# Normalising rows inside the mix: ScalarE with a scale and a bias per row in place of VectorE

## What is computed

```
h      = bn2(conv1d(relu(bn1(conv1(x))), 17 taps));  x_conv = relu(h + x)
s      = x @ w_se.T + b_se                       # 3 coordinates of a node
A      = exp(-|s_n - s_m|^2) * adj
x_nmp  = A @ relu(x @ w_msg.T + b_msg)
r, z   = sigmoid(gates of [x_conv, x_nmp] and x)
n      = tanh(gi_n + r * gh_n)
y      = x + (1 - z) * n + z * x
out    = (y - mean(y)) / sqrt(var(y) + 1e-5)     # per node, over 128 features
```

## Time and profile before

| | us |
|---|---|
| median of 3 runs | 320.26 |
| lowest, highest | 319.72, 322.0 |
| the profiled execution | 320.76 |
| its span, first to last instruction | 318.6 |
| PE busy | 300.3 (94%) |
| PE weight loads busy | 240.6 (76%) |
| DVE busy | 251.5 (79%) |
| ACT busy | 155.9 (49%) |
| POOL busy | 31.1 (10%) |
| mean granted TensorE clock | 0.982 of full |

### The profile page before, as it was taken

The page is one execution under the profiler, slowest core; times in us unless marked ns, Lnnn a source line. Parts: engine busy times, 40 slices in busy tenths (PEclk is TensorE's granted clock), DMA queues, the critical chain, the costliest instruction groups (busy, mean ns, idle before and its releaser), DMA issues.

```text
span 318.6 us, 4624 instructions
## 1 busy us (share of the span) xinstructions
PE 300.3 (94%) x1422; PEld 240.6 (76%) x1422; DVE 251.5 (79%) x666; ACT 155.9 (49%) x326; POOL 31.1 (10%) x53
## 2 busy tenths in 40 slices
PE   8669989899999999999999999999999999999990
PEld 6457767778888778888888778888888778888860
DVE  3995869867977996967987996966987996963794
ACT  3753834338775622237775622237776613324345
POOL 3631000000000051000000041000000032000113
PEclk9959999999999999999999999999999999999997
DMA  7500161171210321171210231181210031150002
GB/s 224 214 1 2 65 224 41 66 265 64 69 34 32 103 97 68 69 263 37 80 47 21 88 122 66 66 263 35 66 51 14 32 132 66 44 154 0 0 35 99
DMA packets 12257, 27.23 MB, mean 85 GB/s; under 512 B 1363, under 2 KB 2133, under 8 KB 12117
## 3 DMA queue, kind: packets, MB, share of 16 engines
q1 hardware_dynamic: 12244, 27.08, 25.1%
HBM read 22.88 MB, written 4.19 MB: 85 GB/s over the span
## 4 chain that ended last, share of the span: by engine, by line
PE 81%; DVE 11%; ACT 2%; issue 2%; DMA 2%; POOL 0%; POOLq 0%; SPq 0%; ACTq 0%; DVEq 0%
PE bank L324 78%; DMA xr<-xt_dram 2%; PE bank L516 2%; PE bank L358 1%; DVE V_lo L969 1%; DVE H L1062 1%; DVE first L1096 1%; DVE V_lo L989 1%; DVE hn L1309 1%; DVE xr L1280 0%; DVE xr L1285 0%; ACT hn L745 0%; DVE x_lo L953 0%; DVE first L1102 0%; DVE H L1077 0%
## 5 line engine op out<-in xcount | busy, mean ns | idle before, releaser
L324 PE MATMUL bank<-V_hi,cw_hi 128*128 128x512 f32 x160 | 70.5, 440 | 2.8 <-ACT EF L661 1.4
L324 PE MATMUL bank<-V_lo,cw_hi 128*128 128x512 f32 x160 | 64.9, 406 | 0.0
L324 PE MATMUL bank<-V_hi,cw_lo 128*128 128x512 f32 x160 | 64.6, 404 | 0.0
L324 PE MATMUL bank<-x_hi,w_hl 128*128 128x512 f32 x128 | 47.3, 410 | 1.1 <-DVE x_lo L953 1.1
L324 PEld LDWEIGHTS bank<-V_hi,cw_hi 128*128 128x128 f32 x160 | 30.6, 191 | 11.0 <-issue 2.5
L324 PEld LDWEIGHTS bank<-V_hi,cw_lo 128*128 128x128 f32 x160 | 30.4, 190 | 8.4
L324 PEld LDWEIGHTS bank<-V_lo,cw_hi 128*128 128x128 f32 x160 | 30.5, 190 | 7.1
L324 PE MATMUL bank<-m_hi,w_hl 128*128 128x512 f32 x96 | 35.3, 400 | 0.6 <-DVE m_lo L1047 0.6
L324 PE MATMUL bank<-c_hi,w_hl 128*128 128x512 f32 x96 | 34.9, 396 | 0.0
L631 ACT ACTIVATE m_hi<-bank 128x512 fp32r<-128x512 f32 x16 | 9.6, 599 | 42.4 <-PE bank L324 42.4
L818 POOL TENSOR_TENSOR rstd<-first,pconst 128x4 f32<-128x4 f32 x16 | 3.5, 220 | 269.4 <-DVE first L1102 269.4
(11 more groups left out here) (135 smaller groups left out, 599.0 us busy)
## 6 DMA issues: line engine op xcount, KB each, us to landing
adj<-adj_dram SPq DMA_DIRECT2D x16, 512.0 KB, 4.4
x<-xt_dram SPq DMA_DIRECT2D x16, 256.0 KB, 3.1
xn<-xn_dram SPq DMA_DIRECT2D x16, 256.0 KB, 4.5
out_dram<-xn SPq DMA_DIRECT2D x15, 256.0 KB, 2.1
xr<-xt_dram SPq DMA_DIRECT2D x13, 256.0 KB, 3.5
xn<-wcv_dram SPq DMA_DIRECT2D x1, 1024.0 KB, 7.3
xr<-xt_dram SPq DMA_DIRECT2D x1, 768.0 KB, 6.0
adj<-wsm_dram SPq DMA_DIRECT2D x1, 512.0 KB, 7.8
```

Of the source, the lines that this page charges most:

```text
L324: return nc.tensor.matmul(out, lhs, rhs, start=start, stop=stop, skip_group_check=True)
```

## The change

ACT's function `normalise` takes the count to wait for as its first argument and moves ahead of `mix_stage`. In the mix, DVE's four calls of `normalise` become four calls of `norm_shift` (one small instruction each) at the same places, and ACT normalises chunks 0 and 1 between `weights(5)` and `relu2(0)`, and chunks 2 and 3 between `weights(7)` and `sums_hi(2)`. SP's stores of groups 0 to 2 wait for `act_out_ready`; the counts that the last group's stores wait for are adapted. The last group's gates keep their work and its order.

```diff
--- before.py
+++ after.py
@@ -241,7 +241,7 @@
                 sp.dma_start(adj[:, pair % 2], adj_d[g, pair]).then_inc(adj_loaded[pair % 2], 16)
 
             def store(g, k):
-                sp.wait_ge(out_ready, 4 * g + k + 1)
+                sp.wait_ge(act_out_ready, 4 * g + k + 1)
                 sp.dma_start(out_d[g, :, NB * k:NB * k + NB, :],
                              xn[:, NB * k:NB * k + NB, :]).then_inc(out_stored[k], 16)
 
@@ -249,15 +249,15 @@
                 def rows(a, b):
                     return out_d[g, :, a:b, :], xn[:, a:b, :]
 
-                sp.wait_ge(out_ready, 4 * g + 1)
+                sp.wait_ge(out_ready, 1)
                 sp.dma_start(*rows(0, NB)).then_inc(out_stored[0], 16)
                 for k in (1, 2):
-                    sp.wait_ge(act_out_ready, k)
+                    sp.wait_ge(act_out_ready, 4 * g + k)
                     sp.dma_start(*rows(NB * k, NB * k + NB)).then_inc(out_stored[k], 16)
                 k = NC - 1
-                sp.wait_ge(out_ready, 4 * g + 2)
+                sp.wait_ge(out_ready, 2)
                 sp.dma_start(*rows(NB * k, NB * k + 2)).then_inc(out_stored[k], 16)
-                sp.wait_ge(act_out_ready, 3)
+                sp.wait_ge(act_out_ready, 4 * g + 3)
                 sp.dma_start(*rows(NB * k + 2, NB * k + NB)).then_inc(out_stored[k], 16)
 
             def load_adj_late(g, pair):
@@ -664,6 +664,15 @@
             def relu2(g, c):
                 act.wait_ge(t_ready, 4 * g + c + 1)
                 nc.scalar.activation(phase(c_hi, c), inner(c), ACT.Relu).then_inc(chi_ready, 1)
+
+            def normalise(n, k, js=range(NB)):
+
+                act.wait_ge(shift_ready, n)
+                for j in js:
+                    at = NB * k + j
+                    last = nc.scalar.activation(xn[:, at, :], xn[:, at, :], ACT.Identity, bias=shift[:, k, j:j + 1],
+                                                scale=rstd[:, at:at + 1])
+                last.then_inc(act_out_ready, 1)
 
             def mix_stage(g, first):
                 if first:
@@ -702,24 +711,21 @@
                 weights(g, 5)
                 if first:
                     slot_high(F3, F_one, slot_diff, 4)
+                else:
+                    normalise(4 * g - 3, 0)
+                    normalise(4 * g - 2, 1)
                 relu2(g, 0)
                 weights(g, 6)
                 shared(g, 2, first)
                 relu2(g, 1)
                 weights(g, 7)
+                if not first:
+                    normalise(4 * g - 1, 2)
+                    normalise(4 * g, 3)
                 sums_hi(g, 2)
                 relu2(g, 2)
                 sums_hi(g, 3)
                 relu2(g, 3)
-
-            def normalise(g, k, js=range(NB)):
-
-                act.wait_ge(shift_ready, k)
-                for j in js:
-                    n = NB * k + j
-                    last = nc.scalar.activation(xn[:, n, :], xn[:, n, :], ACT.Identity, bias=shift[:, k, j:j + 1],
-                                                scale=rstd[:, n:n + 1])
-                last.then_inc(act_out_ready, 1)
 
             def gru_stage(g, last):
                 for k in range(NC):
@@ -754,9 +760,9 @@
                             half = slice(h * N, (h + 1) * N)
                             nc.scalar.activation(z[:, k % 2, half], z_bank[:, half], ACT.Tanh, bias=v(BZ),
                                                  scale=0.5).then_inc(z_ready, 1)
-                        normalise(g, 1)
-                        normalise(g, 2)
-                        normalise(g, 3, (2, 3))
+                        normalise(4 * g + 1, 1)
+                        normalise(4 * g + 2, 2)
+                        normalise(4 * g + 3, 3, (2, 3))
 
             act.wait_ge(first_loaded, 16)
             nc.scalar.activation(w_hi[:, 0, :], w_first, ACT.Copy).then_inc(whi_ready, 1)
@@ -1213,8 +1219,8 @@
                 sums_lo(g, 0)
                 norm(norm_mean, 2)
                 norm(norm_mean, 3)
-                norm(normalise, prev, 0)
-                norm(normalise, prev, 1)
+                norm(norm_shift, prev, 0)
+                norm(norm_shift, prev, 1)
                 if first:
                     slot_low(E3, E_all[:, 3], 4)
                     slot_low(F2, F_one, 5)
@@ -1224,7 +1230,7 @@
                 for k in range(NC):
                     dve.wait_ge(x_loaded[k], 16 * g + 16)
                 conv_sum(g, 0, first)
-                norm(normalise, prev, 2)
+                norm(norm_shift, prev, 2)
                 sums_lo(g, 1)
                 product(g, 1, 1, first)
                 mask(g, 5)
@@ -1234,7 +1240,7 @@
                 conv_sum(g, 1, first)
                 conv_lo(g, 0)
                 mask(g, 6)
-                norm(normalise, prev, 3)
+                norm(norm_shift, prev, 3)
                 if first:
                     setup_taps_lo(3, 7).then_inc(cw_ready, 1)
                 sums_lo(g, 2)
```

## The result

| | before | after |
|---|---|---|
| median, us | 321.13 (319.72 to 322.15, 4 runs) | 327.02 (326.49 to 327.5, 4 runs) |
| ratio to before, 95% interval | | 1.0184 [1.0153, 1.0215] |
| profiled execution, us | 320.76 | 327.5 |
| its span, us | 318.6 | 324.9 |
| DVE / ACT busy, us | 251.5 / 155.9 | 239.6 / 173.3 |

The changed kernel is 1.8% slower: some 5.9 us, between 4.9 and 6.9. The forecast was 326.2, with a span of 324.5.

A forecast was written before the change was run, and what follows sets the result against it. PE, full and without waits in the three later mixes, was taken as the bound; two new waits and a restart cost 3 x 1.96 = 5.9 us, span 318.6 to 324.5, plus 1.66 gives 326.2 us, range 322.8 to 328.4 (0.80).

The forecast's parts named there:

- first burst delays no one: ACT, chunks 0 and 1 behind weights(5): relu2(0) moves from 125.41 to 127.8, covered by DVE's own work; costs nothing.
- loss in a mix, with the restart: PE at m, each later mix: 142.32 - 140.46, plus 0.1 us for a slower next matmul after the wait; 1.96 us.
- What bounds: Later mixes: PE busy 32.00 of 32.00 us, so the 3.6 us a mix taken from DVE earn nothing.
- hidden pace-setter on DVE: Rival: removing 3.6 us from DVE lets PE move up by that in each mix; 309.5 us, chance 0.03.
- The place: ACT's idle 3.64 us ahead of relu2(2) swallows the second burst for relu2(2) alone, not for sums_hi(2); sums_lo(2) 2.81 us late.
- The slack: Second burst ahead of sums_hi(2): it would have to take 1.4 us or less to cost PE nothing.
- absorbed burst: Rival: late sums_hi(2) stays under the slack, so no change; 320.3 us, chance 0.04.
- Both waits: PE in each later mix waits 0.85 us for mask(7) at gather(7), then 1.0 us for the last m_lo.
- one-wait rival: Rival: DVE makes good what mask(7) lost; PE loses 0.85 + 0.1 us a mix, +2.9 us, 323.1; chance 0.09.
- The price of the burst: Eight ACTIVATE on ACT take 3.35 us, as in the final chunk, and push what is behind by 3.25 us.
- cheap burst: Low end of range: ACT runs rows as fast as DVE, burst 2.11 us, loss 0.8 us a mix, 322.7 us.
- The clock: Rival: PE's waits lower the granted clock to 0.66 for 4 us, 1.4 us a mix more; 330.4 us, chance 0.04.

The follow-up runs named there:

- first burst alone: Changed kernel with chunks 2 and 3 normalised by DVE again, only chunks 0 and 1 by ACT behind weights(5); ratio to before 1.0005, about +0.2 us.
- split burst: Changed kernel with chunk 2's four blocks ahead of sums_hi(2) and chunk 3's four behind it; ratio to before 1.0043, about +1.4 us.
- second burst alone: Changed kernel with chunks 0 and 1 normalised by DVE again, only chunks 2 and 3 by ACT ahead of sums_hi(2); ratio to before 1.0161, about +5.2 us.
- burst of twelve: Changed kernel with four more ACTIVATE of the same form behind the second burst's eight, ahead of sums_hi(2); ratio to before 1.0364, about +11.7 us.
- burst behind sums_hi(2): Changed kernel with sums_hi(2) moved ahead of the second burst of eight row blocks on ACT; ratio to before 1.0009, about +0.3 us.
- sums_lo(2) later: Changed kernel with DVE's sums_lo(2) moved behind mask(7) and conv_sum(2) in the later mixes; ratio to before 0.9985, about -0.5 us.

## Why the prediction was right

Its steps for the second mix beside what came. The measured times have the 0.43 us of the start taken off.

| step | predicted | measured |
|---|---|---|
| first burst delays no one | 0 | 0 (first burst alone: 1.0005) |
| second burst begins | 131.88 | 132.17 |
| sums_hi(2) begins | 135.1 | 135.25 |
| sums_lo(2) begins | 135.75 | 135.86 |
| gather(7) begins, late by | 138.35, 0.85 | 138.46, 0.96 |
| conv_lo(2) begins | 139.60 | 139.72 |
| last sums_lo begins | 141.58 | 141.72 |
| m begins | 142.32 | 142.45 |
| m begins, late by | 1.86 | 1.99 |
| loss in a mix, with the restart | 1.96 | 1.93, 1.92 (third, fourth) |
| loss in three | 5.9 | 5.84 |

The restart of 0.1 us behind a wait falls into the next mix's distance, so the 1.99 of the second mix stands against the 1.86.

- *What bounds.* "PE has no idle time to give back" held: DVE lost 11.9 us of work and none of it came back. The rival of a hidden pace-setter on DVE falls.
- *The place.* That relu2(2)'s idle time does not cover sums_hi(2) is shown from both ends, by moving the burst and by moving the instruction that waits.
- *The slack.* The prediction put the burst that costs nothing at 1.4 us. The split burst of 1.55 us lost 0.44 us a mix, of which 0.1 is the restart, so the threshold lies near 1.2: 1.4 was a little too kind. The rival of the absorbed burst would have needed three blocks.
- *Both waits.* The one-wait rival (2.9 us) falls by the timeline: PE waits twice in each mix, 0.6 to 0.8 us and 0.76 to 0.77 us of idle time.
- *The price of the burst* was mis-sized by a little. The eight took 3.18 us and pushed what is behind by 3.08, not 3.35 and 3.25. The row of the final chunk had been read as eight blocks back to back, and they are not. ACT's timeline of before at 311.4 to 311.8, then ACT's and DVE's at 312.2 to 312.6:

```profile
311.15 0.87 ACT L720 ACTIVATE xn<-xn,shift,rstd 128x128 f32<-128x128 f32 x2
...
311.92 1.05 ACT L720 ACTIVATE xn<-xn,shift,rstd 128x128 f32<-128x128 f32 x2
312.27 0.16 DVE L1116 SCALAR_TENSOR_TENSOR shift<-first,rstd 128x4 f32<-128x4 f32 x1
```

The fourth block and the fifth together take 1.05 us where a pair takes 0.87: the fifth is the first of the next chunk, whose shift DVE finishes at 312.43, and begins at 312.47. So 0.17 us of the 3.35 was a wait for DVE, and after the change the same wait is there (shift from 318.65 to 318.81, fifth block at 318.85). The estimate from the Trainium skill ("ScalarE: Activation LUTs", section "What ACT_TABLE_LOAD costs"), 3.19 us for eight, agrees with the 3.18 measured in the mix, and one block with its two operands, 0.48 us by it, had 0.486 in the mean.

- *Luck.* This error was covered by another. In the second mix the burst began 0.29 us later than predicted, since shared(2) did, and in the third 0.10 later; PE's matmuls around it were not late. With both put in, the predicted 1.86 becomes 1.86 - 0.17 + 0.29 = 1.98, and 1.99 was measured; with the burst's true price alone it would be 1.69, and 1.79 in the later mixes. The second burst alone, where shared(2) comes on time within 0.03 us, bears that out: it loses 1.74, 1.82 and 1.88 us. So the agreement to 0.1 us in three mixes is partly luck, and the chain by itself is good to 0.1 us a mix. Shared(2) is late by 0.28 to 0.36 us in the second mix of the five kernels that keep the first mix as it was and have all 16 blocks on ACT, and on time where either burst is left to DVE. What holds it stays open. It also means that "first burst delays no one" is shown for the first burst alone, not for both together.
- *The range* has a small slip: its low end, 322.8, lies above the 322.7 of its own cheap burst, since the scatter was added at the top alone. Nothing hangs on it.
- *ACT's busy time* rose by 17.4 us, where 20 was named as a sign; the price above is part of it.
- *SP.* The loads of xn began at 136.45, or 136.0 without the offset, where 135.9 was predicted, and nobody waited.
- *The clock* did not fall in the changed kernel (0.984 overall, and 1.00 in the stretches around both waits). The rival's price was low: it took the 4 us at 0.66 of the earlier trace rows, and in the 4 us behind them, 20 to 24, the granted clock before was 0.50.

## What to carry over

An engine's idle time ahead of an instruction is room for work only for that instruction; ask of each one behind the insertion when it is wanted, and what stands in its user's queue behind the wait. Where queues run in order, either move of two helps: the inserted work behind the urgent instruction, or the waiting one behind those that are urgent; each costs one line. And go on one step past the wait that was repaired: here the next one, for x_lo, took back 0.4 us. A row that stands for several instructions can hold a wait inside it; before it is used as a price, take it apart.

## What was not expected of the hardware

**The clock fell once for a short wait.** In the kernel with the burst of twelve PE waits 2.34 us for mask(7) in the second mix. Its timeline there:

```profile
140.60 2.06 PE L324 MATMUL bank<-xr,msg 128*128 128x256 f32 x4 [2.34 <-DVE xr L1051]
142.10 0.99 PE L324 MATMUL bank<-x_hi,w_hl 128*128 128x512 f32 x1
```

The matmul of 128x512 behind the gather takes 0.99 us, where it takes 0.58 in the changed kernel. In the third mix of the same execution it looks like this:

```profile
216.96 1.13 PE L324 MATMUL bank<-xr,msg 128*128 128x256 f32 x4 [2.15 <-DVE xr L1051]
217.74 0.58 PE L324 MATMUL bank<-x_hi,w_hl 128*128 128x512 f32 x1
```

The stretches (us; PE, PEld, DVE, ACT, POOL busy; granted clock; DMA share; GB/s):

```profile
138.00:142.00 4.00, 1.66 (x5) 1.15 (x4) 3.30 (x6) 0.64 (x1) 0.00 (x0) 0.83 0.87 196
142.00:146.00 4.00, 4.00 (x15) 3.17 (x14) 3.19 (x5) 1.75 (x3) 0.00 (x0) 0.74 0.78 300
146.00:150.00 4.00, 4.00 (x19) 3.23 (x18) 0.69 (x1) 1.14 (x3) 0.00 (x0) 1.00 0.04 16
212.00:216.00 4.00, 2.81 (x12) 1.87 (x10) 1.64 (x3) 2.33 (x6) 0.00 (x0) 1.00 0.66 223
216.00:220.00 4.00, 3.04 (x13) 2.38 (x13) 3.26 (x6) 1.19 (x2) 0.00 (x0) 1.00 0.91 320
```

PE was busy 1.66 of 4 us, and the granted clock was 0.83 and then 0.74, each a mean over the stretch of its two levels, 2.4 GHz (1.00) and 1.2 GHz; it was full again from 146. In the third and fourth mix PE waited 2.15 us too; in the third it was busy 2.81 and 3.04 us of such stretches, and the clock stayed full. So a fall after waits of this size comes in one mix of three here. This mix lost 4.24 us against 3.34 and 3.45 in the others. About 0.7 us of that is the clock: from the gather to the first matmul with m PE took 4.68 us, against 3.99 in each of the other two. The other 0.2 is the late shared(2): the gather began 2.50 us after it was due and not 2.31. Waits can bring the clock down, as the prediction's rival said, but at the changed kernel's waits of under 1 us nothing of it is seen. Before the change, the clock was down to 0.66 in the stretch at 16 to 20 us, in which PE was busy 1.45 of 4 us.

**The scatter of runs sits in the start.** Eight of the eleven kernels profiled have the first mix as it was. In their executions PE's first matmul with m of the first mix comes between 68.06 and 69.29 us. In the four among them where PE has no new wait (before, burst behind sums_hi(2), first burst alone, sums_lo(2) later) the distance from there to the fourth mix agrees to 0.02 us per mix (72.34, 72.36, 72.34, 72.34), and all that follows that first matmul to 0.11 us (250.54, 250.52, 250.50, 250.43), while the spans differ by a whole microsecond (318.6 to 319.6). A change of half a microsecond in a mix is read from that distance in one profile; from whole runs it takes many.
